# Two blocks in flight between the layers, gathered rows weighted on ScalarE, token tiles transposed three pairs ahead

## The reference

```python
# T = 2048 tokens of 128 columns, all f32
x = x + _L0_attn_ref(_layernorm(x), ...)   # 8 heads over all tokens
x = x + _L0_ffn_ref(_layernorm(x), ...)    # 64 experts, top 6 a token, and a shared expert
x = x + _L1_attn_ref(_layernorm(x), ...)   # no attention matrix: a lookup
x = x + _L1_ffn_ref(_layernorm(x), ...)    # 8 experts, top 2 a token

def _L1_attn_ref(x, W_off, b_off, W_attn, b_attn, W_out, b_out):
    off = (x @ W_off + b_off).reshape(Bx, Nx, H, P, 2)
    w = softmax((x @ W_attn + b_attn).reshape(Bx, Nx, H, P), axis=-1)
    idx = clip(off[..., 0].astype(int32), 0, C - 1)     # a negative one has C added first
    g = take_along_axis(x[:, 0, :], idx.reshape(Bx, -1), axis=1)
    s = sum(g * w, axis=(2, 3))
    return broadcast_to(s[..., None], (Bx, Nx, C)) @ W_out + b_out
```

## Time and profile before

| | us |
|---|---|
| median of three runs (lowest to highest) | 1053.69 (1052.11 to 1057.41) |
| the profiled execution, its own time | 1054.79 |
| its span | 1053.0 |
| PE busy in the span | 744.9 (71%) |
| DVE busy | 691.4 (66%) |
| ACT busy | 442.8 (42%) |
| POOL busy | 393.6 (37%) |

### The profile page before, as it was taken

One profiled execution on the slowest core, in us unless ns is written; L12 is line 12 of the kernel. 1 busy time (PEld: TensorE's weight loads), 2 busy tenths in 40 slices (PEclk: granted clock), 3 DMA queues, 4 the chain that ended last, 5 costly groups with the idle time before them and its releaser, 6 DMA issues.

```text
span 1053.0 us, 18639 instructions
## 1 busy us (share of the span) xinstructions
PE 744.9 (71%) x5996; PEld 431.5 (41%) x5996; DVE 691.4 (66%) x1389; ACT 442.8 (42%) x570; POOL 393.6 (37%) x505
## 2 busy tenths in 40 slices
PE   3533699989998998945757778850456365199992
PEld 2201222322232232222547777740233242199992
DVE  5688899999999999936335554323665754334442
ACT  1350388867876876830213333320100101155550
POOL 5000000024423621646423333337765733635553
PEclk9855699999999999976979999985565566589997
DMA  4999999999991100151464444422111101123335
GB/s 134 279 279 279 279 339 334 283 282 288 286 301 38 44 4 7 44 133 37 154 234 120 121 121 123 133 79 53 48 52 41 49 30 40 49 38 46 53 51 135
DMA packets 79485, 143.17 MB, mean 136 GB/s; under 512 B 10320, under 2 KB 73136, under 8 KB 77632
## 3 DMA queue, kind: packets, MB, share of 16 engines
q1 hardware_dynamic: 55088, 119.33, 38.7%
q0 software_dynamic: 12784, 17.40, 7.4%
q10 hardware_dynamic: 11520, 5.25, 1.9%
HBM read 116.76 MB, written 101.34 MB: 207 GB/s over the span
## 4 chain that ended last, share of the span: by engine, by line
PE 52%; DVE 23%; POOL 8%; issue 7%; DMA 4%; ACT 3%; SPq 1%; POOLq 1%; DVEq 0%
PE PS L518 10%; PE PS L825 6%; PE PS L503 6%; PE PS L493 6%; PE PS L653 5%; DVE PS L1319 4%; PE PS L655 3%; PE PS L835 3%; POOL GB L1110 3%; DVE XQ L1395 3%; POOL slots_scratch L1076 2%; DVE small L1244 2%; DVE hm L1227 2%; DMA XP<-slots_scratch 2%; PE PS L641 2%
## 5 line engine op out<-in xcount | busy, mean ns | idle before, releaser
L903 ACT ACTIVATE PB<-PS 128x1024 f32<-128x1024 f32 x256 | 262.1, 1025 | 116.9 <-PE PS L503 107.7
L1319 DVE TENSOR_SCALAR PS<-PS 128x1024 f32<-128x1024 f32 x256 | 301.6, 1227 | 11.3 <-PE PS L493 7.8
L518 PE MATMUL PS<-PB,VS 128*32 128x256 f32 x2048 | 165.6, 396 | 0.6 <-ACT PB L903 0.6
L1076 POOL DMA_INDIRECT slots_scratch<-XN,slot x96 | 93.7, 976 | 59.8 <-ACT PB L903 38.7
L503 PE MATMUL PS<-QM,KP 64*128 64x512 bf16 x512 | 101.4, 393 | 14.4 <-DVE PS L1319 14.3
L1097 POOL COPY WQ<-W0GU 128x192 f32 x160 | 60.1, 376 | 125.6 <-PE PS L655 97.4
L1110 POOL DMA_INDIRECT GB<-y_scratch,slotc x96 | 91.7, 955 | 36.3 <-issue 28.6
L493 PE MATMUL PS<-QS,KP 64*128 64x512 bf16 x512 | 100.6, 390 | 5.3 <-DVE QM L1261 2.9
L1395 DVE COPY XQ<-PS 128x256 f32<-128x256 f32 x80 | 34.0, 425 | 97.7 <-PE PS L641 97.7
L1085 POOL TENSOR_TENSOR X<-X,TQ 128x256 f32<-128x256 f32 x8 | 5.8, 725 | 220.1 <-DVE TQ L1270 220.1
L653 PE MATMUL PS<-XQ,WQ 128*96 128x128 f32 x320 | 65.9, 288 | 30.6 <-DVE XQ L1395 23.1
(11 more groups left out here) (264 smaller groups left out, 1222.2 us busy)
## 6 DMA issues: line engine op xcount, KB each, us to landing
y_scratch<-YP SPq DMA_DIRECT2D x80, 128.0 KB, 1.8
slots_scratch<-slots_scratch SPq DMA_DIRECT2D x1, 8768.0 KB, 32.6
W0GU<-in_w0gu SPq DMA_DIRECT2D x1, 6144.0 KB, 51.9
XP<-slots_scratch ACTq DMA_DIRECT2D x80, 64.0 KB, 2.1
XP<-slots_scratch SPq DMA_DIRECT2D x80, 64.0 KB, 1.9
W1GU<-in_w1gu SPq DMA_DIRECT2D x1, 4096.0 KB, 13.1
W0D<-in_w0d SPq DMA_DIRECT2D x1, 3072.0 KB, 16.7
XG<-slots_scratch SPq DMA_DIRECT2D x39, 68.5 KB, 2.0
```

The lines of the kernel that those rows point to most:

```text
L518: last = mm(PS[32 * j:32 * j + 32, at + q.start:at + q.stop], VS[:, n, g * HG + j, :], PB[u // 2 % 3][:, 2 * (j % 2) + j // 2, q], start=( ...
L903: A(PB[u // 2 % 3][:, 2 * hp:2 * hp + 2, :], pair_banks(u).rearrange("p (j q) -> p j q", j=2), ACT.Exp).then_inc(sem("exp_done"), 1)
L1076: gp.indirect_dma_start(slots0_dram.rearrange("b p d -> (b p) d"), bass.IndirectOffsetOnAxis(ap=slot0[:, t, k:k + 1], axis=0), XN[:, t, 0: ...
L1319: TS_(pair_banks(u), pair_banks(u), 4.0, 0.0, ALU.mult, ALU.max).then_inc(sem("relu_done"), 1)
```

## The change

**Pairs.** A third `XQ` buffer is put in the memory of `TQ`, which is free by then; a pair is transposed three pairs ahead instead of two. On PE's queue, the turn of a pair i with i = 6k + 2 reads as follows, before and after. `XP` are the loaded tiles, `XQ` and `TQ` the transposed ones, `HP` the hidden rows.

```diff
-        XQ = [sb(f"XQ{i}", [P, 2 * P], f32, experts) for i in range(2)]
+        XQ = [sb(f"XQ{i}", [P, 2 * P], f32, experts) for i in range(2)] + [TQ[:, 0:2 * P]]
...
+        TURN = {(2, 0): 0, (2, 1): 1, (3, 0): 2, (2, 2): 3, (3, 1): 4, (2, 3): 5, (3, 2): 6, (3, 3): 7}
...
             pair_turned(0)
             pair_turned(1)
+            pair_turned(2)
             pair_gates(0)
             for i in range(PAIRS0):
                 experts = pair_experts(i)
                 if i + 1 < PAIRS0:
                     pair_gates(i + 1)
-                if i + 2 < PAIRS0:
-                    pair_turned(i + 2)
+                if i + 3 < PAIRS0:
+                    pair_turned(i + 3)
                 pair_down(i, experts)
...
+            def chunk_turned(l, q, b):
+
+                n = TURN[l, q]
+                pe.wait_ge(sem(f"xn{l}_ready"), q + 1)
+                if l == 3:
+                    pe.wait_ge(sem("ti_ready"), 2 * min(q + 2, NC))
...
+            def fills(q, part):
+                d = 8 * q + 4 * part
+                for kind, i in FILLS[6 * part:6 + 4 * part]:
...
+                    pe.wait_ge(sem("x_lookup"), q)
+                mm(bank(7).rearrange("p (t c) -> p t c", c=P), cf("ones")[0:1, :],
+                   boutb[0:1, :].unsqueeze(1).to_broadcast([1, 4, P]), start=True, stop=False, skip_group_check=True)
+                for m in range(2):
+                    pe.wait_ge(sem("filled_dve"), 8 * q + 7 + m)
+                    for i in range(4):
+                        last = mm(PS[:, 7 * BANK + i * P:7 * BANK + (i + 1) * P], PR[m][:, i * P:(i + 1) * P], cw[:, :],
+                                  start=False, stop=(m == 1), skip_group_check=True)
                 last.then_inc(sem("lookup_psum"), 1)
...
+                chunk_turned(2, q, 0)
                 if q >= 1:
+                    fills(q - 1, 0)
                 offsets(q)
                 if q == 0:
                     tables()
                 else:
+                    fills(q - 1, 1)
+                weights_turned(q)
+                if q >= 1:
+                    lookup(q - 1)
+                if q == NC - 1:
+                    fills(q, 0)
+                if q >= 1:
+                    chunk_turned(3, q - 1, 2)
+                if q == NC - 1:
+                    fills(q, 1)
+                if q >= 1:
+                    router1(q - 1)
+                if q == NC - 1:
+                    lookup(q)
+                if q >= 1:
                     counts1(q - 1)
+            chunk_turned(3, NC - 1, 2)
             router1(NC - 1)
             counts1(NC - 1)
...
+                if i + NXP < PAIRS0:
+                    odd_in(i + NXP)
                 if i >= 1:
                     pair_out(i - 1)
-                if i + NXP < PAIRS0:
-                    odd_in(i + NXP)
             pair_out(PAIRS0 - 1)
...
+            def weighted(q, i):
+                t = 4 * q + i
+                act.wait_ge(sem(f"gathered{t % 4}"), 16 * TOP0 * (t // 4 + 1))
+                if t == 0:
+                    act.wait_ge(sem("weights0_ready"), 1)
+                for k in range(TOP0):
+                    last = A(GB[:, t, k, :], GB[:, t, k, :], ACT.Copy, scale=wtok[:, t, k:k + 1])
+                last.then_inc(sem("weighted"), 1)
+            for i in range(4):
+                weighted(0, i)
             for q in range(NC):
+                more = q + 1 < NC
+                chunk_out(2, q, 0)
                 if q >= 1:
+                    weights_out(q - 1)
+                lookup_exp(q)
+                if more:
+                    weighted(q + 1, 0)
+                lookup_out(q)
+                if more:
+                    weighted(q + 1, 1)
+                else:
+                    weights_out(q)
+                if q >= 1:
+                    chunk_out(3, q - 1, 2)
+                if more:
+                    weighted(q + 1, 2)
                 if q >= 1:
                     router1_exp(q - 1)
+                if more:
+                    weighted(q + 1, 3)
+            chunk_out(3, NC - 1, 2)
             router1_exp(NC - 1)
...
-                gp.tensor_scalar(rstd[:, t], moments[:, t, 1], EPS, None, ALU.add).then_inc(sem("var_chunk"), 1)
-                pool.wait_ge(sem("var_chunk"), q + 1)
-                gp.tensor_tensor(rstd[:, t], rstd[:, t], half[:, t], ALU.pow).then_inc(sem("rstd_chunk"), 1)
+                gp.tensor_tensor(rstd[:, t], moments[:, t, 1], half[:, t], ALU.pow).then_inc(sem("rstd_chunk"), 1)
...
+                gathers(q, 0, 5)
+                chunk_scale(2, q - 1)
+                gathers(q, 5, 22)
                 if q >= 2:
+                    chunk_scale(3, q - 2)
+                gathers(q, 22, 4 * TOP0)
+            chunk_scale(2, NC - 1)
             pool.wait_ge(sem("padded"), 48)
             chunk_dispatch(0)
+            chunk_scale(3, NC - 2)
             chunk_dispatch(1)
+            chunk_scale(3, NC - 1)
...
-                dve.wait_ge(sem(f"gathered{t % 4}"), 16 * TOP0 * (t // 4 + 1))
-                for k in range(TOP0):
-                    step(STT(X[:, t, :], GB[:, t, k, :], wtok[:, t, k:k + 1], X[:, t, :], ALU.mult, ALU.add))
+                dve.wait_ge(sem("weighted"), t + 1)
+                step(v.reduce_sum(mixed[:, :], GB[:, t, :, :].rearrange("p k c -> p c k"), AX.X))
+                step(TT(X[:, t, :], X[:, t, :], mixed[:, :], ALU.add))
                 step(v.bn_stats(stats[:, t, :], X[:, t, :]))
...
+                step(last)
+                TS_(moments[:, t, 1], moments[:, t, 1], EPS, None, ALU.add).then_inc(sem(name), 1)
...
+            for q in range(NC - 1):
+                scaled(2, q)
                 if q >= 1:
+                    filled(q - 1, 0)
+                lookup_index(q)
+                combined(q + 1, 0)
+                if q == 0:
+                    lookup_tables()
+                else:
+                    filled(q - 1, 1)
+                combined(q + 1, 1)
+                if q >= 1:
+                    looked_up(q - 1)
+                    moments_of(q - 1, "moments3")
+                    scaled(3, q - 1)
+                combined(q + 1, 2)
                 if q >= 1:
                     router1_logits(q - 1)
                     router1_chosen(q - 1)
                     router1_slots(q - 1)
+                combined(q + 1, 3)
+                moments_of(q + 1, "moments2")
+            q = NC - 1
+            scaled(2, q)
+            filled(q - 1, 0)
+            lookup_index(q)
+            filled(q - 1, 1)
+            looked_up(q - 1)
+            moments_of(q - 1, "moments3")
+            filled(q, 0)
+            scaled(3, q - 1)
+            filled(q, 1)
+            router1_logits(q - 1)
+            looked_up(q)
+            moments_of(q, "moments3")
+            router1_chosen(q - 1)
+            scaled(3, q)
+            router1_slots(q - 1)
+            router1_logits(q)
+            router1_chosen(q)
+            router1_slots(q)
```

More of the change, by code:

```diff
@@ L1020, in norm_scale @@
                 pool.wait_ge(sem("moments_ready"), 1)
-                gp.tensor_scalar(rstd[:, :], moments[:, :, 1], EPS, None, ALU.add).then_inc(sem("var_ready"), 1)
-                pool.wait_ge(sem("var_ready"), 1)
-                gp.tensor_tensor(rstd[:, :], rstd[:, :], half[:, :], ALU.pow).then_inc(sem("rstd_ready"), 1)
+                gp.tensor_tensor(rstd[:, :], moments[:, :, 1], half[:, :], ALU.pow).then_inc(sem("rstd_ready"), 1)
             gp.memset(half[:, :], -0.5).then_inc(sem("pool_zero"), 1)
@@ L1181, in norm0 @@
                     last = v.bn_aggr(moments[:, t, :], stats[:, t, :])
-                last.then_inc(sem("moments_ready"), 1)
+                step(last)
+                TS_(moments[:, :, 1], moments[:, :, 1], EPS, None, ALU.add).then_inc(sem("moments_ready"), 1)
                 dve.wait_ge(sem("moments_ready"), 1)
@@ L1278, in chunk_stats @@
                 step(last)
-                for t in range(4 * q, 4 * q + 4):
-                    last = v.bn_aggr(moments[:, t, :], stats[:, t, :])
-                last.then_inc(sem("moments_chunk"), 1)
+                t = slice(4 * q, 4 * q + 4)
+                for i in range(4 * q, 4 * q + 4):
+                    last = v.bn_aggr(moments[:, i, :], stats[:, i, :])
+                step(last)
+                TS_(moments[:, t, 1], moments[:, t, 1], EPS, None, ALU.add).then_inc(sem("moments_chunk"), 1)
             def chunk_scores(q):
@@ L1506, in lookup_tables, with filled @@
                 last.then_inc(sem("tables_ready"), 1)
-            def filled(q):
-                for d in range(8):
+            def filled(q, part):
+                for d in range(4 * part, 4 * part + 4):
                     n = 8 * q + d
```

126 lines of the change are left out of this document (39 added, 87 removed).

## The result

The changed kernel takes **1067.02 us** (median of four runs, 1063.73 to 1068.37) beside 1053.87 for the kernel before (1052.11 to 1057.41): a ratio of 1.0116, 95% interval 1.0081 to 1.0151. It is slower, and by about what was forecast (1063.4). The profiled execution is the quickest of the four: its own time is 1063.73, its span 1061.1 us.

The account below looks back on a forecast made before the run. Bounds: down product and number loads after HP in the loop, one cross-engine chain between layers. 1.7 - 2.2 + 10.4 - 0.2 = +9.7 on 1054.8 gives 1064.5, so median 1063.4 us; own range 1059 to 1067, 8 in 10 1041 to 1070.

Parts of the forecast that it names:

- Loop: Expert loop: the third XQ buffer costs 1.7 us in all, between -1 and +3.
- gates follow HP's end by a fixed time: Expert loop: next gates start about 1.9 us after HP's end, so the turn stays 2.19 us while DVE matches.
- The transposition's wait for XP: Start of expert loop: PE meets the 9.47 us wait one turn earlier, +2.2 us, growing to about 11.5.
- what an early XQ gives the other turns: Expert loop, 28 or so turns without matching: saves 0 to 2 us in all, taken as -0.5.
- Rival B: Expert loop: the 22.4 us of waits on the XQ copy are real and go; whole at 1042 us; chance 18%.
- Up to block 0's norm: Start between the layers: one gather and one small POOL operation fewer before the first rstd, -1.5 us.
- Turns: Between the layers, block 0's first norm to block 3's: 31.2 + 43.5 + 43.5 = 118.2 us for 118.9, gaining 0.7.
- the sum, taken at 0.95: DVE's strided reduction of 768 elements in `combined`, between the layers: 0.95 us each.
- Rival D: Between the layers: strided sum at twice 0.95 us, eight sums cost 7.6 more; whole 1071; sign over 1.3; chance 8%.
- The waits for ACT: Full turns between the layers: DVE waits while ACT weights the next tile, 1.9 us, twice in the chain.
- Tail: Block 3's first norm to last scatter: 65.7 us for 55.4, +10.4, as two blocks' fills and lookups lie behind it.
- Rival C: Between the layers: TensorE stays at the faster clock, making 17 us less; whole at 1046.5 us; chance 17%.

Follow-up runs that it names:

- fifth experiment: The changed kernel itself, unaltered, timed again on a second chip without DVE gaps: 1067.7 us beside 1056.4 for the kernel before, ratio 1.0108.
- fourth experiment: Kernel before with only the two expert number loads put behind the next pair's gates: 1151.2 us beside 1132.0, ratio 1.0166.
- sixth experiment: Changed kernel with the two expert number loads put behind the next pair's gates: 1058.7 us, ratio 1.0039 to the kernel before.
- first experiment: Kernel before with the pair change alone (third XQ buffer, transposition three pairs ahead, ACT's pair load ahead of its result copy): 1129.7 us beside 1132.0, ratio 0.9976.
- tenth experiment: Changed kernel with the sum reading six side-by-side values instead of six 512 bytes apart (result no longer the reference's): 1067.7 us in one run.
- seventh experiment: Changed kernel with ACT weighting tiles 1 and 2 of the next block right behind tile 0: 1060.9 us, ratio 1.0042 to the kernel before.
- third: Changed kernel with the weighting back on DVE (six STT a tile), on a chip with DVE gaps: 1105.3 us beside 1132.0 for the kernel before, ratio 0.9760.
- ninth experiment: Changed kernel with the weighting back on DVE (six STT a tile), on a chip without DVE gaps: 1064.6 us beside 1055.3 for the kernel before, ratio 1.0084.
- twelfth: Changed kernel with numbers behind gates, second layer's weights in 16 pieces, earlier weighting, last turn reordered: 1037.1 us beside 1055.3 for the kernel before, ratio 0.9842.
- eleventh: Kernel before, old order, with pairs three ahead, numbers behind gates, weighting on ACT, second layer's weights in 16 pieces: 1032.9 us beside 1055.3, ratio 0.9785.

## Why the prediction was right, and where it missed

- **Direction and size.** Forecast 1063.4, measured 1067.0; the 8 in 10 range was 1041 to 1070. Against the profiled execution the sum said 1064.5 and 1063.7 came. That this is so close is luck in part: the touched stretches cost 10.9 and not 9.7, and the untouched ones were 2.8 shorter in this execution. The median of the runs lies 3.3 above it. The fifth experiment, 11.5 by the same account, bears out the size. There was luck inside the tail as well, told below.
- **Loop: +1.7 forecast, -0.7 measured.** That gates follow HP's end by a fixed time was read rightly. After the change HP ends at 604.55 and the next gates start at 606.36, 1.81 later, for 1.87. In 38 turns with matching the median is 1.84, before the change 1.88:

```profile
604.14 0.41 DVE L1485 TENSOR_TENSOR HP<-PS,SP 96x256 f32<-96x256 f32 x1
605.50 0.61 PE L672 MATMUL PS<-W0D,HP 96*128 x4
606.36 0.43 PE L656 MATMUL PS<-XQ,WQ 128*96 128x128 f32 x2 [0.25 <-DVE XQ L1443]
```

  But the prediction has the down product execute in between, as it waits for HP. In the steady loop the array does not wait there: the down product starts 0.95 us behind HP's end, right behind the transposition. From its end to the next gates it is anything from 0.2 to 0.8 us, while from HP's end it is between 1.68 and 2.07 in all 38 turns. So what HP's end releases is most likely the sequencer, which then loads the numbers while the array still works off what stands before; no record shows the loads themselves. The fourth experiment confirms the loads in part (XQ to gates is 0.06 us when the copy is last), the sixth in full. The transposition's wait for XP was met a turn earlier and grew from 9.47 us to 11.45, and the stretch took +1.9 for +2.2. The term that was too small is what an early XQ gives the other turns, 2.7 us for 0.5. The pairs alone gave 1.0 of that in the first experiment; where the rest comes from was not separated. Rival B would have given -20 and fell.
- **Up to block 0's norm: -1.5 forecast, -1.6 measured.** One gather and one POOL operation fewer.
- **Turns: -0.7 forecast, +1.7 measured.** The gather-bound first piece came at 31.3 for 31.2, the two full turns at 44.6 for 43.5. The mis-sized step is the sum, taken at 0.95 where it takes 1.44. The tenth experiment shows that the stride does it, and that the first turn falls by 1.9 without it. Four sums a turn at 0.49 are 2.0; the turn came out only 1.1 above the forecast, so other steps of my row were 0.9 too dear. Rival D put the limit at 1.3 us a sum and the whole at 1071. By that sign D came, and it had been given 8%: its mechanism is there, at half its price (0.49 a sum for 0.95). By the rule of the Trainium skill ("SBUF — State Buffer", the note on cachelines) an access that goes to a new line each time pays a penalty; the trace agrees, with 1443 ns against 950. The waits for ACT that the forecast had in the chain (two weightings a turn, 1.9 each) were there as 2.9 and 3.6 us, and the seventh experiment took 3.6 off a turn.
- **Tail: +10.4 forecast, +11.6 measured.** This is where the loss is. It stayed with the weighting taken back (67.1 and 67.0 in the third and ninth experiments), with pairs and weighting improved (64.9 in the twelfth), and it is not there under the old order with the same weighting (55.9 in the eleventh). Block 3's moments, ready at 899.63, are 41.0 behind its first norm, which is the forecast to the tenth:

```profile
899.46 0.17 DVE L1509 TENSOR_SCALAR moments<-moments 128x4 f32<-128x4 f32 x1
```

  That is luck in part: block 2's moments came at 22.7 for 25.6, and block 3's looked-up products ended at 34.9 for 34.6, so one part was 2.9 too dear and the next 3.2 too cheap. Behind it the first scatter starts at 45.95 for 45.5, and the 16 scatters take 21.0 for 20.2. Set beside the kernel before, 7.5 of the 11.6 us lie ahead of block 3's second norm (42.1 for 34.7 from its first norm to its second), where two blocks' lookups stand for one. The other 4.1 lie behind it (24.9 for 20.7), where POOL waits 3.83 us for block 2's slots.
- **Rival C, the faster clock between the layers,** fell: 0.61 in the full turns for 0.54 and 0.63, with PE idle 3.5 us ahead of the looked-up products where nearly 5 were forecast. The clock did rise, from 0.64 to 0.71, in the last turn, where the products of blocks 2 and 3 stand close, and the tail was longer all the same. The clock still counts in a turn: the ninth experiment shows 2 to 3 us of it.

## What to carry to other kernels

Software pipelining of two blocks pays by the turns in the middle and costs at the end: count what used to be hidden in the turns and now stands alone behind the last one, here 11.6 us against turns that gained nothing (+1.7 as built, 2.3 less with all repairs in). Before a copy is made a turn earlier because a list of waits blames it, look at the distance from its end to the waiting instruction: 0.57 us where 0.06 is possible means that something else is last, here something without a record. And an edit that does nothing alone (the third buffer) may be what makes another one pay (numbers behind the gates, 9 us) or without which that one loses (16.9 us).

## What the runs showed of the hardware

- The number loads of TensorE's sequencer leave no record of their own and hold back whatever stands behind them: the gates in the kernel before (1.88 us from HP's end, the median of 38 turns), the transposition once they were moved (1.42 us behind the gates' start, in the fourth experiment). This is inferred from the distances and from the sixth experiment, where the turn fell from 2.17 to 1.94 us. The Trainium skill ("TensorE: Matmul & The Clock Gate", section on the array's architecture) gives this engine a queue of 64; the trace shows no run-ahead of these loads past the wait for HP that stands before them.
- A VectorE sum of 128x768 elements to 128x128 takes 950 ns from side-by-side values and 1443 ns from values 512 bytes apart.
- Loads of 4 and 2 MB issued ahead of the small ones kept a small one back for 11.5 us; the same bytes as 16 pieces spread between the small loads left 0.9 us as the longest wait.
- TensorE ran the same 16 products in 2.05 and in 3.48 us in two turns of one execution (ninth experiment), at a granted clock of 0.94 and of 0.55.
- One of the chips ran the same program 7% slower (1132 for 1055 us), partly with even gaps of about 1.05 us ahead of single VectorE instructions in some stretches. The cause stays open.
